# Two of sixteen row maxima of an attention layer become one VectorE pass over 512 sums, with a Relu on ScalarE

## The reference

```
xn  = layernorm(x)
q, k, v = bitnet_linear(xn, sign(w) per output, scale)      # k, v: 8 heads of 16, used by 4 query heads each
scores = q @ k.T / sqrt(16)                                  # 32 heads x 1024 x 1024
attn   = softmax(scores, axis=-1);  out = attn @ v
y   = bitnet_linear(out, ...)
ffn = (silu(xn @ gate.T) * (xn @ up.T)) @ down.T             # 1792 hidden
result = x + y + ffn
```

## Time and profile before

| | |
|---|---|
| median of three runs | 503.11 us |
| profiled execution, its time | 502.01 us |
| profiled execution, span from the first to the last instruction | 500.3 us |
| TensorE / VectorE / ScalarE / GpSimd busy | 482.1 / 416.9 / 348.3 / 94.6 us |
| mean granted TensorE clock | 0.996 |

### The profile page before, as it was taken

The page is one execution under the profiler, slowest core; times in us unless marked ns, Lnnn a source line. Parts: engine busy times, 40 slices in busy tenths (PEclk is TensorE's granted clock), DMA queues, the critical chain, the costliest instruction groups (busy, mean ns, idle before and its releaser), DMA issues.

```text
span 500.3 us, 10322 instructions
## 1 busy us (share of the span) xinstructions
PE 482.1 (96%) x4186; PEld 163.9 (33%) x4186; DVE 416.9 (83%) x487; ACT 348.3 (70%) x655; POOL 94.6 (19%) x138
## 2 busy tenths in 40 slices
PE   1899999999998999999999999999999999999996
PEld 1564444433332222222222222222222233333442
DVE  7879869676777999999999999999999955224986
ACT  1943643352338999999999999999999978874000
POOL 4212244434323000000000000000000113241021
PEclk9999999999998999999999999999999999999999
DMA  8843673732103702102102211211120124452321
GB/s 269 273 95 98 163 151 42 200 74 25 20 1 54 135 24 64 41 24 64 41 24 65 41 36 50 42 57 29 42 63 24 35 78 112 105 148 80 104 84 43
DMA packets 31302, 39.02 MB, mean 78 GB/s; under 512 B 6608, under 2 KB 20816, under 8 KB 31256
## 3 DMA queue, kind: packets, MB, share of 16 engines
q1 hardware_dynamic: 22232, 27.34, 18.9%
q0 software_dynamic: 8304, 10.95, 11.9%
q10 hardware_dynamic: 720, 0.08, 0.1%
HBM read 33.24 MB, written 10.35 MB: 87 GB/s over the span
## 4 chain that ended last, share of the span: by engine, by line
PE 94%; DVE 3%; ACT 1%; DMA 1%; issue 1%; ACTq 0%; SPq 0%; DVEq 0%
PE ps L1319 28%; PE ps L1135 19%; PE ps L1250 15%; PE ps L1144 10%; PE ps L1211 5%; PE ps L1198 5%; PE ps L1114 4%; PE ps L1353 3%; PE ps L1286 2%; DVE stats L768 1%; ACT room L709 1%; DVE room L790 1%; PE ps L1106 1%; PE ps L1155 1%; DMA hlo<-x 1%
## 5 line engine op out<-in xcount | busy, mean ns | idle before, releaser
L842 DVE TENSOR_REDUCE nmx<-ps 128x1 f32<-128x1024 f32 x248 | 284.1, 1216 | 14.2 <-PE ps L1144 13.9
L709 ACT ACTIVATE room<-ps 128x512 f32<-128x512 f32 x512 | 271.5, 602 | 21.5 <-PE ps L1286 11.0
L1319 PE MATMUL ps<-room,vcur 128*32 128x256 f32 (+1 forms) x1880 | 159.6, 411 | 0.7 <-ACT room L709 0.7
L1144 PE MATMUL ps<-kA,qst 48*128 48x512 f16 x496 | 142.4, 384 | 0.0
L1250 PE MATMUL ps<-qst,kB 50*128 50x512 f16 x432 | 135.6, 385 | 0.6 <-DVE room L941 0.4
L1135 PE MATMUL ps<-room,wf 128*128 128x512 f16 x448 | 100.6, 379 | 0.0
L1319 PEld LDWEIGHTS ps<-room,vcur 128*32 128x32 f32 x1880 | 37.2, 108 | 94.6 <-issue 53.9
L689 ACT ACTIVATE room<-ps,gsc 128x512 f32<-128x512 f32 x28 | 19.3, 688 | 61.8 <-PE ps L1135 61.8
L1135 PEld LDWEIGHTS ps<-room,wf 128*128 128x128 f16 x448 | 42.4, 98 | 55.1 <-issue 7.2
L1250 PEld LDWEIGHTS ps<-qst,kB 50*128 50x128 f16 x432 | 27.7, 93 | 92.6 <-ACT room L709 71.9
L546 POOL TENSOR_TENSOR hlo<-room,hhi 128x512 f16<-128x512 f32 x28 | 34.0, 1216 | 87.2 <-ACT hhi L619 87.2
(11 more groups left out here) (136 smaller groups left out, 319.4 us busy)
## 6 DMA issues: line engine op xcount, KB each, us to landing
qst<-q_scratch SPq DMA_DIRECT2D x32, 192.0 KB, 3.6
o_scratch<-osb SPq DMA_DIRECT2D x16, 256.0 KB, 2.3
q_scratch<-parts SPq DMA_DIRECT2D x12, 256.0 KB
hlo<-x SPq DMA_DIRECT2D x8, 256.0 KB, 4.6
parts<-x POOLq DMA_DIRECT2D x8, 256.0 KB, 3.9
wf<-gate POOLq DMA_DIRECT2D x14, 128.0 KB, 3.8
wf<-up POOLq DMA_DIRECT2D x14, 128.0 KB, 5.9
wd<-down POOLq DMA_DIRECT2D x1, 1792.0 KB, 13.5
```

Source lines behind the costliest of these rows:

```text
L709: nc.scalar.activation(probs[:, s % 2, r, :], ps[:, bank_of(gp, s, i), :], ACT.Exp, scale=gam_reg[par][r]).then_inc(scores_free, 1)
L842: nc.vector.tensor_reduce(nmx[:, hf, idx:idx + 1], bank_pair(idx % 2), AX.X, ALU.max, negate=True).then_inc(rows_free, 1)
L1144: return nc.tensor.matmul(ps[:, 2 * (idx % 2) + b, :], qst[low:low + KROWS, par, hf, head, qt * P:(qt + 1) * P], kA[low:low + KROWS, par, ...
L1319: mm = nc.tensor.matmul(ps[32 * r:32 * r + 32, values_bank(step_ // TT), of], vcur[:, par, key_tile(r, j), :], probs[:, s % 2, r, of], sta ...
```

## The change

In the steps with `j` = 4 and `j` = 6 below step 108 (`PAIRED`), the first unit is made in another way; this is 2 of the 16 units of a block, and 26 units in all. Bank 0 holds no longer the products with the first half of the keys, but with half the difference of the two halves (first minus second), from the new buffer `kD`. ScalarE computes twice the positive part of it, `Relu(2 x)`, into the SBUF buffer `excess`; and VectorE adds bank 1 to it, negates, and takes the minimum, in one pass over 512 elements (`row_max_paired`), since max(a, b) = b + max(a - b, 0). The Relu stands right after the first exponential of such a step. It waits for the matmul that makes bank 0 (`excess_due`) and for the paired pass before it; the pass waits for the Relu (`excess_ready`) and for the unit.

The differences of the keys are computed once, on GpSimd, in four operations between those of the first stage (`difference`), and stored to DRAM in three parts; SyncE loads them again, one more DMA of 48 x 512 for each key head (seven in all). TensorE has as many matmuls as before, of the same shapes.

```diff
+    PAIRED = [4, 6]
+    def paired(step):
+        return step < LATE and step % TT in PAIRED
...
# SyncE
+            def load_differences(g, par):
+                sp.dma_start(kD[0:KROWS, par, :],
+                             d_scratch[bass.ds(g, 1)].rearrange("g t d n -> (g t d) n")).then_inc(kD_loaded[par], 16)
...
+            sp.wait_ge(diff_ready, 1)
+            for term, part in enumerate([0, 0, 1]):
+                sp.dma_start(d_scratch[:, term], diff_parts[:, part, :]).then_inc(diff_stored, 16)
             sp.wait_ge(sign_wo_ready, 1)
...
+            sp.wait_ge(diff_stored, 16 * TERMS)
+            sp.wait_ge(abs_wo_ready, HC)
+            load_differences(1, 1)
             load_shift(0, 0, 0)
...
                         load_keys(kA, kA_loaded, g + 2, par)
+                        load_differences(g + 2, par)
# GpSimd: difference(0) ahead of the loop over w, difference(1) to (3) at w = 4, 5, 6
+                    nc.gpsimd.tensor_tensor(diff, y[:, 0, 0:HALF], y[:, 0, HALF:T], ALU.subtract).then_inc(diff_step, 1)
...
+                    nc.gpsimd.tensor_scalar(diff, diff, k_down[:, 0:1], 0.5, ALU.mult, ALU.mult).then_inc(diff_step, 1)
...
+                    nc.gpsimd.tensor_copy(diff_parts[:, 0, :], diff).then_inc(diff_step, 1)
...
+                    nc.gpsimd.tensor_tensor(diff_parts[:, 1, :], diff, diff_parts[:, 0, :],
+                                            ALU.subtract).then_inc(diff_ready, 1)
# ScalarE, in exps
                     nc.scalar.activation(probs[:, s % 2, r, :], ps[:, bank_of(gp, s, i), :], ACT.Exp,
                                          scale=gam_reg[par][r]).then_inc(scores_free, 1)
+                    if i == 0 and paired(step):
+                        act.wait_ge(excess_due, pairs_before(step) + 1)
+                        before = [p for p in range(step) if paired(p)]
+                        if before:
+                            act.wait_ge(rows_free, 2 + 2 * UNITS + 2 * before[-1] + 1)
+                        nc.scalar.activation(excess, ps[:, 0, :], ACT.Relu, scale=2.0).then_inc(excess_ready, 1)
# VectorE
+            def row_max_paired(n, hf, idx, pairs):
+                dve.wait_ge(rows_ready, n + 1)
+                dve.wait_ge(excess_ready, pairs + 1)
+                nc.vector.tensor_tensor_reduce(gr[:, 0:HALF], ps[:, 1, :], excess, -1.0, TOP, ALU.add, ALU.min,
+                                               nmx[:, hf, idx:idx + 1]).then_inc(rows_free, 1)
...
+                    dve.wait_ge(diff_step, 1)           # before the projection of v overwrites y
...
+                    if paired(step):
+                        row_max_paired(ga_ * (2 * UNITS) + hf * UNITS + 2 * j, hf, 2 * j, pairs_before(step))
+                    else:
+                        row_max(ga_ * (2 * UNITS) + hf * UNITS + 2 * j, hf, 2 * j)
                     row_max(ga_ * (2 * UNITS) + hf * UNITS + 2 * j + 1, hf, 2 * j + 1)
# TensorE, in scores
+                        if i == 0 and paired(step):
+                            assert half == 1
+                            pe.wait_ge(kD_loaded[1 - par], 16 * ((gp_ * 2 + par + 2) // 2))
+                            mm = half_rows(1 - par, hf, idx, 0, kD)
+                            mm.then_inc(excess_due, 1)
+                        else:
+                            mm = half_rows(1 - par, hf, idx, 1 - half)
```

More of the change, by code:

```diff
@@ L28, in layer_kernel @@
 def layer_kernel(nc, x, wq, wk, wv, wo, wq_rows, wk_rows, wv_rows, wo_rows, sq, sk, sv, so, gate, up, down, sg, su, sd, out,
-                 q_scratch, k_scratch, o_scratch, r_scratch):
+                 q_scratch, k_scratch, d_scratch, o_scratch, r_scratch):
     T, H = x.shape
@@ L112, in layer_kernel, with pairs_before @@
     LATE = (NG - 1) * STEPS - 4
+    PAIRED = [4, 6]
+    def paired(step):
+        return step < LATE and step % TT in PAIRED
+    def pairs_before(step):
+        return sum(paired(s) for s in range(step))
     RING = [4, 5, 6, 7]
@@ L204, in layer_kernel @@
         oparts = room1[:, 0:QT * T].bitcast(F16).rearrange("p (t a n) -> p t a n", t=QT, a=2)
+        diff = room1[:, 0:HALF]
+        diff_parts = room1[:, HALF:2 * HALF].bitcast(F16).rearrange("p (a n) -> p a n", a=2)
+        kD = room1[:, QT * T:QT * T + HALF].bitcast(F16).rearrange("p (a n) -> p a n", a=2)
+        excess = room1[:, QT * T + HALF:QT * T + 2 * HALF]
         sgn = sb("sgn", [P, HC, NQKV], F16)
@@ L327, in layer_kernel @@
         kA_loaded = [sem(f"kA_loaded{a}") for a in range(2)]
+        diff_step = sem("diff_step")
+        diff_ready = sem("diff_ready")
+        diff_stored = sem("diff_stored")
+        kD_loaded = [sem(f"kD_loaded{a}") for a in range(2)]
+        excess_due = sem("excess_due")
+        excess_ready = sem("excess_ready")
         kB_loaded = [sem(f"kB_loaded{a}") for a in range(2)]
@@ L554, in split_max, with difference @@
                 nc.gpsimd.tensor_tensor(shp[:, hf, 1, :], mxs[:, :], shp[:, hf, 0, :], ALU.subtract).then_inc(shift_ready, 1)
+            def difference(stage):
+                if stage == 0:
+                    pool.wait_ge(sign_ready, 3)
+                    pool.wait_ge(guarded, 2)
+                    nc.gpsimd.tensor_tensor(diff, y[:, 0, 0:HALF], y[:, 0, HALF:T], ALU.subtract).then_inc(diff_step, 1)
+                elif stage == 1:
+                    pool.wait_ge(diff_step, 1)
+                    pool.wait_ge(out_factors_ready, 1)
+                    nc.gpsimd.tensor_scalar(diff, diff, k_down[:, 0:1], 0.5, ALU.mult, ALU.mult).then_inc(diff_step, 1)
+                elif stage == 2:
+                    pool.wait_ge(diff_step, 2)
+                    nc.gpsimd.tensor_copy(diff_parts[:, 0, :], diff).then_inc(diff_step, 1)
+                else:
+                    pool.wait_ge(diff_step, 3)
+                    nc.gpsimd.tensor_tensor(diff_parts[:, 1, :], diff, diff_parts[:, 0, :],
+                                            ALU.subtract).then_inc(diff_ready, 1)
+            difference(0)
             for w in range(FU):
@@ L559, in _ @@
                     split_max(0, 0)
+                if 4 <= w < 7:
+                    difference(w - 3)
                 if hf == 0 and 1 <= f <= FT - WF_BUFS:
@@ L963, in step_rows @@
                 if step < LATE:
-                    row_max(ga_ * (2 * UNITS) + hf * UNITS + 2 * j, hf, 2 * j)
+                    if paired(step):
+                        row_max_paired(ga_ * (2 * UNITS) + hf * UNITS + 2 * j, hf, 2 * j, pairs_before(step))
+                    else:
+                        row_max(ga_ * (2 * UNITS) + hf * UNITS + 2 * j, hf, 2 * j)
                     row_max(ga_ * (2 * UNITS) + hf * UNITS + 2 * j + 1, hf, 2 * j + 1)
@@ L1138, in feed_forward, with half_rows @@
                 mm.then_inc((gate_ready, up_ready)[z], 1)
-            def half_rows(par, hf, idx, b):
+            def half_rows(par, hf, idx, b, keys=None):
                 head, qt = idx // (HALF // P), idx % (HALF // P)
                 low = b * HI
+                keys = kA if keys is None else keys
                 return nc.tensor.matmul(ps[:, 2 * (idx % 2) + b, :],
                                         qst[low:low + KROWS, par, hf, head, qt * P:(qt + 1) * P],
-                                        kA[low:low + KROWS, par, :], start=True, stop=True)
+                                        keys[low:low + KROWS, par, :], start=True, stop=True)
             def rows(n, par, hf, idx):
@@ L1256, in scores @@
                             pe.wait_ge(rows_free, (gp_ * 2 + par + 1) * (2 * UNITS) + hf * UNITS + idx + 1)
-                        mm = half_rows(1 - par, hf, idx, 1 - half)
+                        if i == 0 and paired(step):
[3 more added lines that the diff above has]
+                            mm.then_inc(excess_due, 1)
+                        else:
+                            mm = half_rows(1 - par, hf, idx, 1 - half)
                         if i % 2 == 1:
@@ L1414 @@
     args.append(nc.dram_tensor("k_scratch", (NKV, 3, D, T), F16, kind="Internal").ap())
+    args.append(nc.dram_tensor("d_scratch", (NKV, 3, D, T // 2), F16, kind="Internal").ap())
     args.append(nc.dram_tensor("o_scratch", (NH * 2 * D, T), F32, kind="Internal").ap())
```

## The result

The changed kernel takes 512.29 us (median of six runs, 511.78 to 515.76) against 502.89 us for the one before (median of six): 1.0187 times as long, 95% interval 1.0152 to 1.0222. It is slower by 9.4 us, clear of no change. The forecast was 512.2 us.

The account below looks back on a forecast made before the run. The prediction took TensorE as the bound, tied closely to ScalarE's exponentials. To the median of 503.1 us it added 9.1 for ScalarE, 0 for VectorE and 0 for the first stage and queues: 512.2 us, range 507 to 521.

Parts of the forecast that it names:

- The bound: Attention blocks: TensorE's own 1.11 us per half step, plus transpose and waits for ScalarE, sets the 18.2 us block.
- The term for ScalarE: Steps 4 and 6: the added Relu delays the last exponential, so TensorE waits 0.35 us per pair, +9.1 us in all.
- over before the next pair: ScalarE is back in its old place by step 5's third exponential, so the 0.35 us is not paid twice.
- The term for VectorE: Paired pass waiting for the Relu: costs 0, at most +14 us.
- the edge: Second unit's banks after the paired pass: no cost while pass plus small instruction take up to 0.78 us; estimated 0.71 to 0.80.
- The first stage and the queues: GpSimd's four added operations and SyncE's added stores and loads: cost 0, at most +1.7 us.
- VectorE as the true pace: Rival, attention blocks: freed banks set TensorE's pace, so relieving VectorE wins 3.4 us, to 499.7 us; chance 8%.
- A cheaper ScalarE: Rival, steps 4 and 6: the Relu costs only 0.05 to 0.19 us per pair, 504.4 to 508 us; chance 10%.
- a dear pass: Rival: paired pass with its small instruction takes over 0.78 us, freeing banks late; 518 us at 1.0, 526 at 1.32; chance 20%.
- table loads: Rival, attention: Relu needs another table than Exp, two 1.28 us loads per pair, 67 us in all, 570 us; chance 1%.

## Why the prediction was right

**The bound.** TensorE's 1.11 us per half step as its own pace, with ScalarE's waits on top, is shown by three runs: relief of VectorE gives nothing (18.21), relief of both gives 17.99 (17.96 was worked out), load on VectorE shows at once beyond 0.13 us (0.12 was read).

**The term for ScalarE**, 26 x 0.35 = 9.1: measured 26 x 0.34 = 8.8 by the blocks. Its three numbers held: 0.48 us to the next operation (measured 0.48), the last exponential long by 0.63 to 0.66 when ScalarE runs back to back (the values follow its start by 0.68), 0.14 of slack at that place (0.13 to 0.14 by the small Relu). That it is over before the next pair is right for two pairs that are two steps apart: both their half steps are 1.45 us. For neighbours it is not, as four pairs show. That the time came within 0.1 us of the forecast is partly luck: the medians differ by 9.4 us and the blocks by 8.8, the rest lies within what the runs differ by, and the base that I added to was 0.2 above the later median.

**The term for VectorE**, 0: right in the sum and not in its parts. The pass with its second instruction occupies VectorE for 0.61 us (278.93 to 279.54), since the reading of the accumulator overlaps entirely with the next reduction, where I had 0.71 to 0.80. But the handover from the Relu is 0.14 to 0.15 us, not 0.05. The second unit's banks, where I had seen the edge, were free just in time (279.54 + 1.22 = 280.76, wanted at 280.88). But I looked only at that pair of banks; the first unit's own banks are wanted earlier, at the first `half_rows` of the next step, and come 0.25 us late. That this cost nothing, because ScalarE's 0.34 covers it, is luck and not foresight. The run with the Relu first agrees: there the banks come in time, and the block is shorter by only 0.03 per pair. Without ScalarE's part this wait would perhaps be the next one; no run shows that.

**The first stage and the queues**, 0: right, 139.46 us against 139.47.

**The rivals.** VectorE as the true pace fell with the two runs without Relus. A cheaper ScalarE and a dear pass fell in the profile itself (0.34 per pair; 0.69 us for the pass). The profile after has three table loads, as before, the last 1.41 us ahead of the first exponential and none between the exponentials. This agrees with what the Trainium skill says of relu (ScalarE: Activation LUTs, Table sets: the hidden batching unit). Its rule that a saturated VectorE may be relieved to ScalarE (Perfetto Trace Analysis, Optimizing Scalar/DVE Operations) did not carry here, because VectorE was full without being the pace.

**The single pair.** It costs 0.38 and not the 0.34 that I had expected, and the second adds 0.29; the profile shows why. With one pair (copies at 266.88 and 285.48), VectorE and TensorE after the pass:

```profile
276.05 10.27 DVE L899 TENSOR_REDUCE nmx<-ps 128x1 f32<-128x1024 f32 x9
...
280.71 0.39 PE L1319 MATMUL ps<-qst,kB 50*128 50x512 f16 x1
280.72 0.60 PE L1213 MATMUL ps<-kA,qst 48*128 48x512 f16 x2
...
281.25 0.64 PE L1394 MATMUL ps<-room,vcur 128*32 128x256 f32 x8
281.82 0.39 PE L1319 MATMUL ps<-qst,kB 50*128 50x512 f16 x1
281.85 0.58 PE L1213 MATMUL ps<-kA,qst 48*128 48x512 f16 x2
...
282.38 0.64 PE L1394 MATMUL ps<-room,vcur 128*32 128x256 f32 x8
...
283.52 0.64 PE L1394 MATMUL ps<-room,vcur 128*32 128x256 f32 x8
```

The half step of the pair is 1.45 us, as in the changed kernel: 0.34. But in the last four half steps before the copy TensorE goes at 1.13 us, VectorE's own distance ((10.27 - 1.22)/8 = 1.131), and `half_rows` starts 0.03 behind its score. VectorE waited 0.85 us for the Relu, which is more than the pass saves it (1.13 - 0.61 = 0.52), then ran without a gap, and its small lead was used up. Those four make 0.08, and the half step with the copy is 1.17 in place of 1.21: 0.34 + 0.08 - 0.04 = 0.38. In the changed kernel no half step is 1.13 long. Even with one pair the first four half steps behind it are 1.11, and in the changed kernel no more than four come before the next pair or the copy. So there the second pair adds its 0.34 and takes away those 0.04. Why the copy's half step is shorter wasn't looked into.

## What to carry to other kernels

An engine that is busy in every slice is not thereby the pace: compare the distance between its starts with the distance of the engine it feeds. Before work is moved to an engine with idle time, ask which of its results is waited for most tightly, and how much later that one becomes; its slack at that place (0.14 us here), not its idle time over a block (some 0.7 us), is what is free, and the same work behind the fourth exponential instead of the first costs less than half. And look at each buffer that the moved work holds, beginning with the one that is wanted first. The engine that is relieved can lose too: if its shorter instruction has to wait for the helper, the wait can be longer than what it saves.

## What was not expected of the hardware

- The two-input pass with a reduction over 128 x 512 (one input from PSUM, one from SBUF, float32) lasts 0.69 us and leaves VectorE free after 0.61; the reading of its accumulator (0.08) starts with the next reduction and adds nothing.
- A Relu of 128 x 512 on ScalarE is followed by the next operation after 0.48 us if it reads PSUM and after 0.52 if it reads SBUF; one of 128 x 128 from PSUM after 0.15.
- VectorE starts 0.14 to 0.15 us after the Relu it waits for has ended, while TensorE starts 0.05 after an exponential's end.
